# Ten value units as rounded halves and rests in place of four, and a new order of the last units

## The chip, the cores and the metric

The kernel runs on one core of a Trainium2 chip. The metric is device time in microseconds (us), here the median of several executions. The engines of the core each work through their own list of instructions and wait for one another by semaphores: TensorE (PE in the profile, its weight loads PEld), VectorE (DVE), ScalarE (ACT), GpSimd (POOL) and SyncE (SP), which here only issues DMAs.

## The reference

Self-attention over an image of 4 batches, 128 channels and 1024 positions, all in float32:

```
def _L0_conv_ref(x, gn_w, gn_b, qw, qb, kw, kb, vw, vb, pw, pb):
    h = _group_norm(x, gn_w, gn_b)                 # 8 groups
    q = jnp.einsum('oc,bcn->bon', qw, h) + qb[None, :, None]
    k = jnp.einsum('oc,bcn->bon', kw, h) + kb[None, :, None]
    v = jnp.einsum('oc,bcn->bon', vw, h) + vb[None, :, None]
    attn = jnp.einsum('bcn,bcm->bnm', q, k) / jnp.sqrt(jnp.asarray(C, x.dtype))
    attn = jax.nn.softmax(attn, axis=-1)
    out = jnp.einsum('bnm,bcm->bcn', attn, v)
    out = jnp.einsum('oc,bcn->bon', pw, out) + pb[None, :, None]
    return x + out.reshape(B, C, H, W)
```

## The kernel before, in words

The 4096 query positions are cut into 32 **chunks** of 128, eight to a batch. For chunk c, TensorE makes the scores against all 1024 keys of its batch (L329 to L333; both operands are split into a rounded half and a rest, hi and lo, so that one product takes three passes of the faster kind: hi by hi, hi by lo, lo by hi). VectorE copies them out of PSUM and finds the minimum of each row (L703, "drain"), ScalarE takes the exponential (L524), and the probabilities must then be transposed before they can be multiplied by v. For chunks 0, 1, 30 and 31 TensorE transposes them (L426). For the others VectorE transposes blocks of 32 by 32 (L712), and DMAs put the blocks in their places: a **set** of four chunks (`SETS`; sets 1 to 7) is moved by 16 DMAs of 128 KB from `blocks` to `pT` (L196), four for each of four groups a. The semaphore `moved[...][a]` counts the four of a group.

A moved set is multiplied by v in four **value units**. Units 0 and 1 make the first 256 columns (groups a = 0, 1), from key tiles 0 to 3 and 4 to 7; units 2 and 3 the other 256 (a = 2, 3). I write (n, u) for unit u of set n. A whole unit is four matmuls of 256 columns in float32 (L399), each of which the trace shows as two records. Sets 2, 4 and 6 cross from one batch to the next and are cut otherwise; their units are eight matmuls of 128 columns. In the main loop unit number m runs after the scores of chunk m + 8 (`LAG`). In this kernel (3, 2), (3, 3), (5, 2) and (5, 3) are **rounded units**: v and the probabilities are split into hi and lo, and twelve faster matmuls take the place of the four (L370 to L372). The halves come from ScalarE, which casts (`round_v` L533, `round_probs` L543), the rests from GpSimd, which subtracts (`split_v` L864, `split_probs` L872). `p_hi` and `p_lo` have room for two units.

After the loop, TensorE ends with units 23 to 25, the rden broadcast, (7, 0), (7, 1), then chunks 30 and 31 together in two direct units (L357), then (7, 2), (7, 3) (L473 to L480). VectorE multiplies each finished sum by the inverse denominators (`divide` L732, `finish_last_moved` L745 and L750, `add_residual` L738) and SP stores the rows. All of SP's transfers, the moves, the spreading of the inverse denominators and the stores, stand in one order (L225 to L237): for each set its move, its spread, and the store of the set two before.

## Time and profile before

| what | us |
|---|---|
| median of three runs | 140.52 (139.68 to 140.91) |
| the profiled execution | 139.28 |
| its span | 137.0 |
| TensorE busy | 128.5 (94%) |
| VectorE busy | 100.8 (74%) |
| ScalarE busy | 70.4 (51%) |
| GpSimd busy | 40.4 (29%) |

The span is what the trace covers; the profiled execution's own time is 2.28 us more. Busy time is an average over parts of the program with different limits. The chain of waits follows the end of the program back, from each piece of work to what released it.

### The profile page before, as it was taken

To read this page: it belongs to the slowest core of one execution; us is meant where nothing else is said; L and a number is where in the kernel's file an instruction comes from.
4 is the path that set the end of the run, shared out by engine and by line. 5 is a ranking of instruction groups with operands and counts; after the bars stand their busy time and mean duration, and the time that the engine had idled before them with its cause. 6 is when DMAs were issued, how large, how long until landed. Compare 5 with 4: busy or idle time off the path is not lost.

```text
span 137.0 us, 2258 instructions
## 1 busy us (share of the span) xinstructions
PE 128.5 (94%) x759; PEld 111.9 (82%) x759; DVE 100.8 (74%) x172; ACT 70.4 (51%) x118; POOL 40.4 (29%) x39
## 2 busy tenths in 40 slices
PE   5999999997877999999999999999999999999990
PEld 5897888884556888989898898899988999998870
DVE  0577789989999678979689989856987798240222
ACT  4053789655556574637357796475576335321000
POOL 5053050750202033303324696015039412003000
PEclk9999999999999999999999999999999999999999
DMA  4960000003998599869672898799835997999412
GB/s 139 288 263 0 0 5 0 10 31 67 202 212 195 136 208 208 181 150 208 136 188 105 195 212 196 221 206 208 198 105 120 199 209 219 237 206 199 153 38 77
DMA packets 9566, 21.00 MB, mean 153 GB/s; under 512 B 2362, under 2 KB 4052, under 8 KB 9556
## 3 DMA queue, kind: packets, MB, share of 16 engines
q1 hardware_dynamic: 8816, 20.59, 61.7%
q10 hardware_dynamic: 740, 0.28, 0.8%
q8 instruction: 6, 0.10, 0.3%
q14 instruction: 4, 0.03, 0.1%
HBM read 4.07 MB, written 2.11 MB: 45 GB/s over the span
## 4 chain that ended last, share of the span: by engine, by line
PE 84%; DVE 8%; issue 3%; DMA 2%; SPq 0%; DVEq 0%
PE ACC L399 31%; PE S L329 10%; PE S L330 9%; PE S L333 9%; PE A L309 5%; DVE s_sb L703 3%; PE S L357 3%; PE ACC L357 3%; DMA x_sb<-x 2%; PE S L273 2%; DVE blocks L712 2%; PE ACC L371 1%; DVE bn L628 1%; PE ACC L372 1%; PE ACC L370 1%
## 5 line engine op out<-in xcount | busy, mean ns | idle before, releaser
L703 DVE TENSOR_SCALAR_CACHE_REDUCE s_sb<-S,row_term 128x1024 f32<-128x1024 f32 x32 | 40.9, 1279 | 13.9 <-PE S L333 13.7
L399 PE MATMUL ACC<-pT,v 128*128 128x128 f32 (+1 forms) x288 | 45.8, 310 | 0.0
L524 ACT ACTIVATE s_sb<-s_sb,rowmin 128x1024 f32<-128x1024 f32 x32 | 36.9, 1152 | 15.6 <-DVE s_sb L703 14.1
L399 PEld LDWEIGHTS ACC<-pT,v 128*128 128x128 f32 x288 | 40.3, 191 | 3.2 <-issue 0.4
L712 DVE STREAM_TRANSPOSE blocks<-s_sb 128x1024 f32<-128x1024 f32 x28 | 34.7, 1239 | 0.0
L329 PE MATMUL S<-h_hi,g_hi 128*128 128x512 f32 x64 | 28.5, 446 | 0.3 <-issue 0.3
L330 PE MATMUL S<-h_lo,g_hi 128*128 128x512 f32 x64 | 25.1, 393 | 0.0
L333 PE MATMUL S<-h_hi,g_lo 128*128 128x512 f32 x64 | 19.9, 392 | 0.0
L857 POOL TENSOR_TENSOR xb<-rden_bc,xb 128x512 f32<-128x512 f32 (+1 forms) x7 | 8.4, 1200 | 26.5 <-DVE rden_bc L732 18.9
L333 PEld LDWEIGHTS S<-h_hi,g_lo 128*128 128x128 f32 x64 | 12.0, 188 | 2.8
L329 PEld LDWEIGHTS S<-h_hi,g_hi 128*128 128x128 f32 x64 | 12.1, 189 | 2.1 <-issue 0.4
L330 PEld LDWEIGHTS S<-h_lo,g_hi 128*128 128x128 f32 x64 | 12.1, 189 | 1.7
L872 POOL TENSOR_TENSOR p_lo<-pT,p_hi 128x1024 fp32r<-128x1024 f32 x4 | 9.6, 2403 | 10.2 <-ACT p_hi L543 10.2
L516 ACT COPY v<-A 128x384 f32<-128x384 f32 (+1 forms) x12 | 5.3, 443 | 14.2 <-PE A L309 14.2
L309 PEld LDWEIGHTS A<-wpv,h 128*128 128x128 f32 x64 | 8.4, 190 | 3.7 <-issue 2.6
L309 PE MATMUL A<-wpv,h 128*128 128x129 f32 x64 | 9.5, 281 | 1.3 <-DVE g_lo L677 1.2
L844 POOL TENSOR_TENSOR h_lo<-h,h_hi 128x1024 fp32r<-128x1024 f32 x3 | 7.2, 2402 | 11.7 <-ACT h L494 11.7
L504 ACT ACTIVATE g_hi<-A,wpv 128x512 fp32r<-128x512 f32 x7 | 4.8, 689 | 9.2 <-PE A L291 9.2
L273 PE MATMUL S<-ident 128*128 128x128 f32 x38 | 7.3, 343 | 1.6 <-POOL ident L877 1.6
L864 POOL TENSOR_TENSOR v_lo<-v,v_hi 128x1024 fp32r<-128x1024 f32 x2 | 4.7, 2368 | 12.8 <-ACT v_hi L533 12.8
L835 POOL TENSOR_TENSOR rstd<-gvar,minus_half 128x1 f32<-128x1 f32 x4 | 2.2, 554 | 20.2 <-DVE gvar L650 20.2
L628 DVE BATCH_NORM_STATS2 bn<-x_sb 128x6 f32<-128x512 f32 x8 | 5.3, 684 | 3.2 <-DMA x_sb<-x 3.2
(100 smaller groups left out, 144.7 us busy)
## 6 DMA issues: line engine op xcount, KB each, us to landing
pT<-blocks SPq DMA_DIRECT2D x112, 128.0 KB, 2.4
rden_bc<-row_store SPq DMA_DIRECT2D x6, 256.0 KB, 3.5
x_sb<-x SPq DMA_DIRECT2D x1, 1024.0 KB, 6.4
out<-xb SPq DMA_DIRECT2D x8, 128.0 KB, 2.8
out<-xb SPq DMA_DIRECT2D x4, 256.0 KB, 3.1
x_sb<-x SPq DMA_DIRECT2D x2, 256.0 KB, 3.0
x_sb<-x SPq DMA_DIRECT2D x1, 512.0 KB, 3.8
w_in<-weights ACTq DMA_DIRECT2D x2, 128.0 KB, 3.5
```

What stands on the lines that cost most here:

```text
L273: pe.matmul(S[:, 0, BANK:BANK + P], ident[:, :], ident[:, :], start=True, stop=True)
L309: last = pe.matmul(A1[:, PW1 * u:PW1 * (u + 1)], h[:, P * t:P * (t + 1)], wpv[:, 0:PW1], start=True, stop=True)
L329: pe.matmul(S[:, c % 2, ks], g_hi[:, qs], h_hi[:, b % 2, ks], start=True, stop=False)
L330: pe.matmul(S[:, c % 2, ks], g_hi[:, qs], h_lo[:, b % 2, ks], start=False, stop=False)
L333: last = pe.matmul(S[:, c % 2, ks], g_lo[:, qs], h_hi[:, b % 2, ks], start=False, stop=True)
L357: last = pe.matmul(sums[n], v[:, FIRST[n] // CH % 3, t, :], pair_T[:, t].rearrange("p d q -> p (d q)"), start=(t == 0), stop=(t == KT - 1))
L399: last = pe.matmul(to, v[:, b % 3, t, :], probs[:, :, t, :], start=(t == 0), stop=(t == KT - 1))
L524: act.activation(s_sb[:, c % 3, :], s_sb[:, c % 3, :], ACT.Exp, bias=rowmin[:, c % CH:c % CH + 1], scale=-1.0, accum_out=den[:, n % 2, k:k ...
L703: dve.tensor_scalar(s_sb[:, c % 3, :], S[:, c % 2, :], row_term[:, b % 2, i:i + 1], None, ALU.add, ALU.min, accum_out=rowmin[:, i:i + 1]). ...
L712: dve.transpose(blocks_view(n)[:, :, :, k, :].rearrange("p j t q -> p t j q"), s_sb[:, c % 3, :].rearrange("p (t j q) -> p t j q", t=KT, j ...
L857: pool.tensor_tensor(xs, rden_bc[:, n % 2, 0:P * SETS[n]], xs, ALU.add).then_inc(out_ready, 1)
L872: pool.tensor_tensor(lo, moved_view(n)[:, 2:4, PT * half:PT * (half + 1), :].rearrange("p a t n -> p t a n"), hi.bitcast(F32), ALU.subtrac ...
```

## The change

- The units that are rounded are now listed one by one (`SPLIT_UNITS`): (1, 2), (1, 3), (3, 0) and (5, 0) are new in the loop, (7, 2) and (7, 3) at the end; (3, 2), (3, 3), (5, 2), (5, 3) stay. v is split four times in place of two, by ScalarE after the exponentials of chunks 7, 15, 23 and 30 and by GpSimd a chunk later.
- ScalarE casts for (1, 2) and (1, 3) after the exponential of chunk 10, for (3, 0) and (5, 0) in chunks 17 and 25 ahead of the rounding of g, for (7, 2) and (7, 3) after all its other work. The rests for the last two are made by VectorE, not GpSimd.
- Chunks 30 and 31 get a unit each, of eight matmuls of 128 columns. The end is (7, 0), (7, 1), chunk 30, (7, 2), (7, 3), chunk 31. Each of the two chunks has its own two VectorE operations and its own store.

```diff
 FIRST_UNIT_STEPS = (4, 5)
 LAG = 8
 
-SPLIT_SETS = (3, 5)
+SPLIT_UNITS = ((1, 2), (1, 3), (3, 0), (3, 2), (3, 3), (5, 0), (5, 2), (5, 3), (7, 2), (7, 3))
+
+SPLIT_SETS = (1, 3, 5, 7)
+ROUND_V_STEPS = (7, 15, 23, 30)
+
+BY_DVE = 8
...
+
+    FIRST_QUARTERS = {FIRST[n] + 7: SPLIT_UNITS.index((n, 0)) for n in (3, 5)}
+    SECOND_QUARTERS = {FIRST[n] + 6 + u: SPLIT_UNITS.index((n, u)) for n in (3, 5) for u in (2, 3)}
...
-        sums = [ACC[:, n % 2, 0:P * SETS[n]] for n in range(LS)] + [S[:, 1, 0:PN]]
+        sums = [ACC[:, n % 2, 0:P * SETS[n]] for n in range(LS)]
+
+        chunk_sums = [S[:, 1, BANK * d:BANK * d + P] for d in range(2)]
...
+
+        def split_views(r):
+
+            n, u = SPLIT_UNITS[r]
+            part, half = u // 2, u % 2
+            probs = moved_view(n)[:, 2 * part:2 * (part + 1), PT * half:PT * (half + 1), :].rearrange("p a t n -> p t a n")
+            return (probs, *(p[:, r % 2].rearrange("p t (a n) -> p t a n", a=2) for p in (p_hi, p_lo)))
+
+        def unit_end(r):
+
+            n, u = SPLIT_UNITS[r]
+            return FIRST[n] + u + 1
...
-                    sp.wait_ge(tail_out_ready, 2 if n == LS else 3)
+                    sp.wait_ge(tail_out_ready, 3)
...
+            def store_chunk(d):
+                sp.wait_ge(tail_out_ready, (2, 4)[d])
+                cs = slice(P * (CH - 2 + d), P * (CH - 1 + d))
+                sp.dma_start(out[L, :, cs], xb[:, L, cs]).then_inc(stored, 16)
...
             store_set(LS - 2)
-            store_set(LS)
+            store_chunk(0)
             store_set(LS - 1)
-            sp.wait_ge(stored, 16 * (NS + sum(crosses(n) for n in range(NS))))
+            store_chunk(1)
+            sp.wait_ge(stored, 16 * (NS + 1 + sum(crosses(n) for n in range(NS))))
...
+            def last_chunk_unit(d):
+                for f in range(HALVES):
+                    pe.wait_ge(pair_ready[f], SETS[0] + SETS[LS])
+                pe.wait_ge(v_ready, VP * B)
+                pe.wait_ge(rowmin_ready, STEPS)
+                for t in range(KT):
+                    last = pe.matmul(chunk_sums[d], v[:, L % 3, t, :], pair_T[:, t, d, :], start=(t == 0), stop=(t == KT - 1))
+                last.then_inc(part_done, 1)
+
+            def split_unit(n, u):
+                r, k = SPLIT_UNITS.index((n, u)), SPLIT_SETS.index(n)
+                part, half = u // 2, u % 2
+                if u == 0:
+                    pe.wait_ge(normed_ready, n - 1)
+                if u == 2 and n == LS - 1:
+                    pe.wait_ge(normed_ready, n)
+                pe.wait_ge(v_hi_ready, k + 1)
+                pe.wait_ge(v_lo_ready, k + 1)
+                pe.wait_ge(p_hi_ready, r + 1)
+                if r < BY_DVE:
+                    pe.wait_ge(p_lo_ready, r + 1)
+                else:
+                    pe.wait_ge(last_lo_ready, r - BY_DVE + 1)
+                to = last_sums[part] if n == LS - 1 else sums[n][:, UW * part:UW * (part + 1)]
                 for w in range(PT):
                     t = PT * half + w
-                    pe.matmul(to, v_hi[:, t, :], p_hi[:, half, w, :], start=(t == 0), stop=False)
-                    pe.matmul(to, v_hi[:, t, :], p_lo[:, half, w, :], start=False, stop=False)
-                    last = pe.matmul(to, v_lo[:, t, :], p_hi[:, half, w, :], start=False, stop=(t == KT - 1))
+                    pe.matmul(to, v_hi[:, t, :], p_hi[:, r % 2, w, :], start=(t == 0), stop=False)
+                    pe.matmul(to, v_hi[:, t, :], p_lo[:, r % 2, w, :], start=False, stop=False)
+                    last = pe.matmul(to, v_lo[:, t, :], p_hi[:, r % 2, w, :], start=False, stop=(t == KT - 1))
                 last.then_inc(part_done, 1)
...
             def moved_unit(n, u):
-                if n in SPLIT_SETS and u > 1:
-                    split_unit(n, u - 2)
+                if (n, u) in SPLIT_UNITS:
+                    split_unit(n, u)
                     return
...
-                if n in (0, LS):
-                    direct_unit(n, u)
+                if n == 0:
+                    first_pair_unit(u)
+                elif n == LS:
+                    last_chunk_unit(u)
                 else:
                     moved_unit(n, u)
...
             value_unit(FIRST[LS - 1])
             value_unit(FIRST[LS - 1] + 1)
             value_unit(DIRECT)
-            value_unit(DIRECT + 1)
             value_unit(FIRST[LS - 1] + 2)
             value_unit(FIRST[LS - 1] + 3)
+            value_unit(DIRECT + 1)
...
+            def round_probs(r):
+                n, u = SPLIT_UNITS[r]
+                for a in (2 * (u // 2), 2 * (u // 2) + 1):
+                    act.wait_ge(moved[n % 2][a], MOVED * ((n + 1) // 2))
+                if r > 1:
+                    act.wait_ge(part_done, unit_end(r - 2))
+                    act.wait_ge(p_lo_ready, r - 1)
+                probs, hi, lo = split_views(r)
+                act.copy(hi, probs).then_inc(p_hi_ready, 1)
...
                 if i == 0:
                     copy_v(b, 1)
+                if c in FIRST_QUARTERS:
+                    round_probs(FIRST_QUARTERS[c])
                 if i == 1:
                     round_g(b, 1)
...
-                for k, n in enumerate(SPLIT_SETS):
-                    if c - FIRST[n] in (8, 9):
-                        round_probs(n, c - FIRST[n] - 8)
+                if c in SECOND_QUARTERS:
+                    round_probs(SECOND_QUARTERS[c])
                 exponentials(c)
-                for k, n in enumerate(SPLIT_SETS):
-                    if c == FIRST[n] + 5:
-                        round_v(k)
+                if c in ROUND_V_STEPS:
+                    round_v(ROUND_V_STEPS.index(c))
+                if c == FIRST[1] + LAG:
+                    round_probs(0)
+                    round_probs(1)
             copy_pair(STEPS - 1)
             copy_rden(LS - 1)
             copy_rden(LS)
+            round_probs(BY_DVE)
+            round_probs(BY_DVE + 1)
...
-                dve.wait_ge(part_done, FIRST[n] + SETS[n] if n < LS else STEPS - 2)
+                dve.wait_ge(part_done, FIRST[n] + SETS[n])
...
+            def finish_last_chunk(d):
+                dve.wait_ge(part_done, (STEPS - 3, STEPS)[d])
+                dve.wait_ge(bc_ready, 2)
+                by_rden = rden_bc[:, LS % 2, P * d:P * (d + 1)]
+                dve.tensor_tensor(by_rden, chunk_sums[d], by_rden, ALU.mult).then_inc(chunk_normed, 1)
+                dve.wait_ge(chunk_normed, d + 1)
+                dve.wait_ge(xb_ready, B)
+                xs = xb_flat[:, P * (DIRECT + d):P * (DIRECT + d + 1)]
+                dve.tensor_tensor(xs, by_rden, xs, ALU.add).then_inc(tail_out_ready, 1)
+
+            def split_last_probs(half):
+                r = BY_DVE + half
+                dve.wait_ge(p_hi_ready, r + 1)
+                dve.wait_ge(part_done, unit_end(r - 2))
+                probs, hi, lo = split_views(r)
+                dve.tensor_tensor(lo, probs, hi.bitcast(F32), ALU.subtract).then_inc(last_lo_ready, 1)
...
-                dve.wait_ge(part_done, FIRST[n] + 2 if part == 0 else STEPS)
+                dve.wait_ge(part_done, FIRST[n] + 2 if part == 0 else STEPS - 1)
...
             divide(LS - 2)
+            split_last_probs(0)
             finish_last_moved(0)
-            divide(LS)
-            add_residual(LS)
+            split_last_probs(1)
+            finish_last_chunk(0)
             finish_last_moved(1)
+            finish_last_chunk(1)
...
+            def split_probs(r):
+                pool.wait_ge(p_hi_ready, r + 1)
+                if r > 1:
+                    pool.wait_ge(part_done, unit_end(r - 2))
+                probs, hi, lo = split_views(r)
+                pool.tensor_tensor(lo, probs, hi.bitcast(F32), ALU.subtract).then_inc(p_lo_ready, 1)
...
-                for k, n in enumerate(SPLIT_SETS):
-                    if c == FIRST[n] + 6:
-                        split_v(k)
-                    if c - FIRST[n] in (8, 9):
-                        split_probs(n, c - FIRST[n] - 8)
+                if c - 1 in ROUND_V_STEPS:
+                    split_v(ROUND_V_STEPS.index(c - 1))
+                if c in FIRST_QUARTERS:
+                    split_probs(FIRST_QUARTERS[c])
+                if c in SECOND_QUARTERS:
+                    split_probs(SECOND_QUARTERS[c])
+                if c == FIRST[1] + LAG:
+                    split_probs(0)
+                    split_probs(1)
```

TensorE's rows from the broadcast of the inverse denominators (rden) to its last instruction, before: L399 are whole units of set 7, L357 chunks 30 and 31.

```order
L426 MATMUL A<-ident,s_sb 128x128 x8
L399 MATMUL ACC<-pT,v 128x2x64 x8
L347 MATMUL S<-ident,rden 128x128 x6
L399 MATMUL ACC<-pT,v 128x256 x8
L357 MATMUL S<-pair_T,v 128x256 x8
L399 MATMUL ACC<-pT,v 128x256 x8
```

The same place with the change (L444 are whole units, L395 a chunk, L415 to L417 rounded units).

```order
L473 MATMUL A<-ident,s_sb 128x128 x8
L444 MATMUL ACC<-pT,v 128x2x64 x8
L375 MATMUL S<-ident,rden 128x128 x6
L444 MATMUL ACC<-pT,v 128x256 x8
L395 MATMUL S<-pair_T,v 128x128 x8
L415 MATMUL ACC<-p_hi,v_hi 128x256
L416 MATMUL ACC<-p_lo,v_hi 128x256
L417 MATMUL ACC<-p_hi,v_lo 128x256
...
L395 MATMUL S<-pair_T,v 128x128 x8
```

Chunk 31 has moved behind the two last units of set 7, and these are rounded: the three rows L415 to L417 come eight times.

VectorE's last rows, from the division of set 6's sums, before (L745 and L750 finish a half of set 7, L729 and L738 the two chunks).

```order
L732 TENSOR_TENSOR rden_bc<-ACC,rden_bc 128x4x4x32
L745 TENSOR_TENSOR rden_bc<-ACC,rden_bc 128x2x4x32
L750 TENSOR_TENSOR xb<-rden_bc,xb 128x2x4x32
L729 TENSOR_TENSOR rden_bc<-S,rden_bc 128x256
L738 TENSOR_TENSOR xb<-rden_bc,xb 128x256
L745 TENSOR_TENSOR rden_bc<-ACC,rden_bc 128x2x4x32
L750 TENSOR_TENSOR xb<-rden_bc,xb 128x2x4x32
```

The same with the change (L801 makes a rest, L808 and L813 finish a half of set 7, L790 and L794 a chunk).

```order
L783 TENSOR_TENSOR rden_bc<-ACC,rden_bc 128x4x4x32
L801 TENSOR_TENSOR p_lo<-pT,p_hi 128x1024
L808 TENSOR_TENSOR rden_bc<-ACC,rden_bc 128x2x4x32
L813 TENSOR_TENSOR xb<-rden_bc,xb 128x2x4x32
L801 TENSOR_TENSOR p_lo<-pT,p_hi 128x1024
L790 TENSOR_TENSOR rden_bc<-S,rden_bc 128x128
L794 TENSOR_TENSOR xb<-rden_bc,xb 128x128
L808 TENSOR_TENSOR rden_bc<-ACC,rden_bc 128x2x4x32
L813 TENSOR_TENSOR xb<-rden_bc,xb 128x2x4x32
L790 TENSOR_TENSOR rden_bc<-S,rden_bc 128x128
L794 TENSOR_TENSOR xb<-rden_bc,xb 128x128
```

The first rest stands ahead of the finish of set 7's first half, the second behind it.

ScalarE's rows of chunks 10 to 12 with the change; before, the row of the two casts (L590) is not there.

```order
L571 ACTIVATE s_sb,den<-s_sb,rowmin 128x1024
L590 CAST p_hi<-pT 128x1024 x2
L536 ACTIVATE h_hi<-x_sb,gshift,gscale 128x1024
L571 ACTIVATE s_sb,den<-s_sb,rowmin 128x1024
L541 ACTIVATE h<-x_sb,gshift,gscale 128x1024
```

Both casts stand between the exponential of chunk 10 (L571) and the normalizing for the next batch (L536), which the exponential of chunk 11 follows.

## Rows read from the trace of the kernel before

**Rows 1.** The page, TensorE's busy tenths in 40 equal slices of the span.

```profile
PE   5999999997877999999999999999999999999990
```

**Rows 2.** Chain of waits, 111 to 137 us: start, us, engine and line, records.

```profile
112.17 1.78 PE ACC L399 x16
...
123.09 3.68 PE ACC L399 x16
126.77 3.45 PE S L357 x16
130.22 3.47 PE ACC L399 x16
133.71 0.44 DVE rden_bc L745
...
134.17 0.42 DVE xb L750
```

**Rows 3.** Timeline of SP's queue, 100 to 137 us: start, us, line, operation.

```profile
102.29 10.98 SPq L196 DMA_DIRECT2D pT<-blocks  x16
...
114.96 10.50 SPq L196 DMA_DIRECT2D pT<-blocks  x16
```

**Rows 4.** Timeline of VectorE, 100 to 118 us: transposes of chunks 25 and 29.

```profile
101.02 1.24 DVE L712 STREAM_TRANSPOSE blocks<-s_sb 128x1024 f32<-128x1024 f32 x1
...
113.55 1.24 DVE L712 STREAM_TRANSPOSE blocks<-s_sb 128x1024 f32<-128x1024 f32 x1
```

**Rows 5.** Set 7's moves: seventh and eighth, then fifteenth and sixteenth, with landings.

```profile
L196 SPq DMA_DIRECT2D pT<-blocks x2: 590/596/602, 118.8 to 119.5; - x2
DMA to landing us min/median/max: 2.9/3.2/3.5
...
L196 SPq DMA_DIRECT2D pT<-blocks x1: 592/592/592, 124.9 to 124.9; - x1
DMA to landing us min/median/max: 2.6/2.6/2.6
```

**Rows 6.** Timeline of TensorE, 100 to 118 us: starts of units (5,1), (5,2), (5,3).

```profile
103.28 1.89 PE L399 MATMUL ACC<-pT,v 128*128 128x256 f32 x8
...
106.40 0.28 PE L370 MATMUL ACC<-p_hi,v_hi 128*128 128x256 f32 x1
...
109.20 0.28 PE L370 MATMUL ACC<-p_hi,v_hi 128*128 128x256 f32 x1
```

**Rows 7.** Groups by line and shape: busy us and mean ns, idle before.

```profile
L543 ACT CAST p_hi<-pT 128x1024 fp32r<-128x1024 f32 x4 | 4.2, 1044 | 0.0
L668 DVE TENSOR_TENSOR h_lo<-h,h_hi 128x512 fp32r<-128x512 f32 x2 | 1.4, 709 | 0.4 <-ACT h_hi L489 0.4
```

**Rows 8.** Timeline of all engines, 73.5 to 82 us: start, us, engine, operation.

```profile
73.73 2.39 POOL L872 TENSOR_TENSOR p_lo<-pT,p_hi 128x1024 fp32r<-128x1024 f32 x1 [1.90 <-ACT p_hi L543]
...
74.42 1.72 DVE L661 SCALAR_TENSOR_TENSOR gshift<-neg_mean,gscale,cols 128x1 f32<-128x1 f32 x1
...
78.48 2.42 POOL L872 TENSOR_TENSOR p_lo<-pT,p_hi 128x1024 fp32r<-128x1024 f32 x1 [1.13 <-ACT p_hi L543]
...
81.28 0.28 PE L370 MATMUL ACC<-p_hi,v_hi 128*128 128x256 f32 x1
```

**Rows 9.** Timeline of ScalarE, 43 to 69 us; in brackets the idle time before.

```profile
45.27 1.24 ACT L489 ACTIVATE h_hi<-x_sb,gshift,gscale 128x1024 fp32r<-128x1024 f32 x1 [0.26 <-issue]
47.80 1.15 ACT L524 ACTIVATE s_sb<-s_sb,rowmin 128x1024 f32<-128x1024 f32 x1 [1.28 <-DVE s_sb L703]
...
68.48 0.69 ACT L504 ACTIVATE g_hi<-A,wpv 128x512 fp32r<-128x512 f32 x1 [2.19 <-PE A L291]
```

**Rows 10.** Timeline of SP's queue, 30 to 100 us: the moves of sets 1 and 3.

```profile
31.97 10.12 SPq L196 DMA_DIRECT2D pT<-blocks  x16
...
58.38 11.24 SPq L196 DMA_DIRECT2D pT<-blocks  x16
```

**Rows 11.** Busy time per engine, 34 to 42 us; granted clock, DMA share and GB/s last.

```profile
34.00:42.00 8.00, 6.39 (x30) 4.41 (x28) 7.97 (x16) 4.96 (x10) 0.74 (x1) 1.00 0.95 208
```

More of the change, by code:

```diff
@@ L349, in broadcast_rden, with first_pair_unit @@
                 last.then_inc(bc_psum, 1)
-            def direct_unit(n, half):
+            def first_pair_unit(half):
                 if half == 0:
                     for f in range(HALVES):
-                        pe.wait_ge(pair_ready[f], 2 if n == 0 else 4)
-                    pe.wait_ge(v_ready, VP if n == 0 else VP * B)
+                        pe.wait_ge(pair_ready[f], SETS[0])
+                    pe.wait_ge(v_ready, VP)
                 for t in range(PT * half, PT * (half + 1)):
-                    last = pe.matmul(sums[n], v[:, FIRST[n] // CH % 3, t, :], pair_T[:, t].rearrange("p d q -> p (d q)"),
+                    last = pe.matmul(sums[0], v[:, 0, t, :], pair_T[:, t].rearrange("p d q -> p (d q)"),
@@ L358, in direct_unit @@
                                      start=(t == 0), stop=(t == KT - 1))
                 last.then_inc(part_done, 1)
-            def split_unit(n, half):
-                k = 2 * SPLIT_SETS.index(n) + half
-                pe.wait_ge(v_hi_ready, k // 2 + 1)
-                pe.wait_ge(v_lo_ready, k // 2 + 1)
-                pe.wait_ge(p_hi_ready, k + 1)
-                pe.wait_ge(p_lo_ready, k + 1)
-                to = sums[n][:, UW:2 * UW]
+            def last_chunk_unit(d):
[6 more added lines that the diff above has]
+                last.then_inc(part_done, 1)
@@ L533, in round_v @@
                 act.copy(v_hi[:, :, :], v[:, b % 3]).then_inc(v_hi_ready, 1)
-            def round_probs(n, half):
-                k = 2 * SPLIT_SETS.index(n) + half
-                if half == 0:
-                    for a in (2, 3):
-                        act.wait_ge(moved[n % 2][a], MOVED * ((n + 1) // 2))
-                if k > 1:
-                    act.wait_ge(part_done, FIRST[SPLIT_SETS[k // 2 - 1]] + 2 + half + 1)
-                    act.wait_ge(p_lo_ready, k - 1)
-                act.copy(p_hi[:, half].rearrange("p t (a n) -> p t a n", a=2),
-                         moved_view(n)[:, 2:4, PT * half:PT * (half + 1), :].rearrange("p a t n -> p t a n")).then_inc(p_hi_ready, 1)
+            def round_probs(r):
[7 more added lines that the diff above has]
+                act.copy(hi, probs).then_inc(p_hi_ready, 1)
             def copy_rows(n):
```

18 lines of the change are left out of this document (3 added, 15 removed).

## The prediction, made before the changed kernel ran

> **What bounds the kernel now.** I read the page's busy slices of TensorE first: nine tenths or more in every slice of 3.4 us from 44.5 us to the end of its work, seven or eight in the four before that [rows 1]. The chain of waits over the last 25 us says where this decides: after the scores of chunk 31 it is TensorE alone, value unit after value unit, and then two VectorE operations and a store [rows 2]. So a microsecond taken from TensorE is a microsecond gained wherever TensorE is what everybody waits for, and nothing where it waits itself. The profiled execution took 139.28 us, 2.28 more than its span of 137.0; the median of the three runs is 140.52, 1.24 above it. I make the sum in the trace's own time and add 3.5 at the end.
>
> Two other views matter. The SP queue shows that the moves of set 7 are issued from 114.96 on, directly behind those of set 6 and its other transfers: 102.29 to 114.96, or 12.67 us, of which the moves alone take 10.98; the last blocks of set 7 are ready at 113.55 + 1.24 = 114.79 [rows 3, 4]. SP and VectorE are level there. And the moves' landings: the eighth DMA of set 7 (issued 119.46) lands after 3.5 us, at 122.96; unit 26, which needs the first eight, has its first matmul on the chain at 123.09 [rows 2, 5]. So the moves are already level with TensorE. The sixteenth (issued 124.87) lands after 2.6, at 127.47 [rows 5]; TensorE reaches unit 28, which needs it, only at 130.22. These 2.75 us of slack are what the change spends.
>
> **A rounded unit against a whole one.** Unit and next scores of a whole quarter take 106.40 - 103.28 = 3.12 us; with a rounded one 109.20 - 106.40 = 2.80 [rows 6]. So **0.32 us per unit** on TensorE. Six more are rounded: (1,2), (1,3), (3,0), (5,0) in the loop, (7,2), (7,3) at the end. Each costs ScalarE a cast of 1.04 and a subtraction on GpSimd of 2.4 (at the end: on VectorE) [rows 7, 8]. The two more roundings of v cost the same two instructions, behind the exponentials of chunks 7 and 30. There ScalarE's next work, a copy for TensorE or VectorE, comes up to 1 us later; both have work of their own until then, VectorE at chunk 7 and TensorE at chunk 30, so I count 0, and 1.04 once if that cover fails.
>
> **Loop, early.** (1,2) and (1,3) run after the scores of chunks 12 and 13, in full slices [rows 1]. Their casts stand behind the exponential of chunk 10 and ahead of the h_hi that ScalarE starts at 45.27 [rows 9]; set 1's moves have then landed (issued from 31.97 over 10.12 [rows 10], the last at 41.5, landing by 44.1). The casts put h_hi and the exponential of chunk 11 back: 45.0 + 2 x 1.04 + 1.24 = 48.3, against a start of that exponential at 47.80 [rows 9], so 0.5, of which VectorE, which transposes chunk 11 only after draining chunk 12, sees nothing. I count this at 0 and the saving at 0.64; without the cover it would be the 0.5.
>
> **Loop, sets 3 and 5.** Each first quarter's cast stands before the rounding of g, where ScalarE sits idle 2.19 us before set 3's at 68.48 [rows 9] (set 5 repeats it, two such places in all); 1.04 fits, if the first eight moves have landed, which by start + 8.0 (as in set 7: 114.96 to 122.96) is 66.4 for set 3, against 68.48 - 1.04 = 67.4. The covered cost is 0; without that cover, chunk 17's exponential would be late by up to 1 us. One place is tight. The subtraction for (3,2) already blocks VectorE: the one-column gshift takes 1.72 us beside GpSimd's 2.39, and both end near 76.1 [rows 8]. Behind it stand the cast and subtraction for (3,3), ready at 78.48 + 2.42 = 80.90; TensorE wants it at 81.28 [rows 8]. The first of these subtractions can move up by 0.64 only (chunk 17's gain), TensorE by 0.96: 80.26 against 80.32. That costs 0 to 0.1.
>
> The Trainium skill, "SBUF — State Buffer", section "Who interferes with whom", says that a VectorE instruction with two SBUF inputs waits for a GpSimd one that reads SBUF, and one with a single SBUF input, outside the two-port modes, doesn't. The gshift row agrees with the first half; no row shows g_lo (one input in PSUM) beside a subtraction. By the page the new subtraction at chunk 17 costs g_lo nothing; if it were wrong, g_lo would wait the 0.4 by which the two overlap in my schedule.
>
> So by chunk 26 VectorE is ahead by 3 x 0.32 = **0.96**, by chunk 30 by 1.28.
>
> **Set 7's moves.** Its blocks are ready at 114.79 - 1.28 = 113.51. SP began set 6's moves when chunk 25 was transposed (101.02 + 1.24 = 102.26 [rows 4]), now at 101.33, and needs its 12.67: 114.00. So the moves gain 0.96, TensorE 1.28. Unit 26 waits for the eighth until 122.96 - 0.96 = 122.0. Units 26 and 27 as before, 3.68 [rows 2], to 125.8. Chunk 30 as eight 128-column matmuls: as the eight (16 passes) of 1.78 [rows 2], to 127.6. The two chunks take 3.57 where the pair took 3.45: 0.12 more.
>
> **The end.** Unit (7,2) could start at 127.6. Its cast needs all 16 moves: **L = 127.47 - 0.96 = 126.5** (ScalarE has by then only its two rden copies to make, for which TensorE's part ended at 123.1 - 1.28). From L on the work is serial:
> - cast, 1.04 [rows 7];
> - subtraction on VectorE. No row has it at 1024 columns. Bounds: 1.24, the transpose of 1024 [rows 4], and 2 x 0.709 = 1.42, the 512-column one with both inputs in SBUF doubled [rows 7]. I take 1.25, since the fixed part of an instruction isn't doubled;
> - (7,2) can start: L + 2.4 = 128.9, a **TensorE stall of 1.3**. It ends 1.42 later, at 130.3;
> - but VectorE must first finish the first half of set 7, queued behind the first subtraction: 0.44 + 0.42 [rows 2], then the second subtraction, 1.25: L + 4.55 = 131.0, a second stall of 0.7;
> - unit (7,3) 1.42 (half of the last pair's 3.47 [rows 2] less 0.32), chunk 31 1.79: 134.3;
> - two VectorE operations of 128 columns. The 256-column ones take 0.44 and 0.42; 512 takes 0.709, so 128 columns fewer are 0.14 less: 0.60 with the handoff. VectorE ends at 134.9, where it ended at 134.59;
> - the last store: 137.0 - 134.59 = 2.41, taken unchanged, since nothing shows a 64 KB one. It could be a few tenths less.
>
> In all: handoffs 0.15, L + 1.04 + 1.25 + 0.88 + 1.25 + 1.42 + 1.79 + 0.60 + 2.41 = L + 10.79 = **137.3**, against 137.0: +0.3. What was gained by chunk 26 (0.96), with the two rounded units and the shorter finish, is spent by the wait on the cast and two subtractions. In run time 139.28 + 0.3 = 139.6, at the median **140.8**.
>
> The store of set 7 is issued at about 133.4 and lands before the last. SP's new store of chunk 30 stands before it and waits for VectorE at 131.6, so holds up nothing.
>
> The bounds of L: issue of 16 moves from 10.12 to 11.24 in other sets against 10.50 [rows 3, 10], start between 113.5 (bound by the blocks) and 114.0: L from 125.6 to 127.3. With 0 to 0.3 from the two subtractions that is 136.4 to 138.4, in runs **139.9 to 141.9**: the forecast's own range.
>
> **Rivals.**
> - *The end does not wait.* Were moves, cast and subtraction early enough, TensorE would run through: 122.0 + 3.68 + 1.79 + 2 x 1.42 + 1.79 = 132.1, + 3.01 = 135.1, so -1.9: **138.6**. For it: the end is otherwise pure TensorE, ScalarE and VectorE are idle there, and the landing times are the least sure of my numbers. Against: L must be at most 125.2 for no first stall and 124.5 for no second, 2 us earlier than the trace has it. A half of the way would do for -0.9. 0.18.
> - *Slower: the loop gives nothing by chunk 29.* The new casts sit ahead of exponentials, and subtractions beside gshift. If the casts of chunks 10, 17 and 25 put back VectorE's transposes by 0.32 each, the 0.96 is gone, VectorE and SP start set 7's moves at 114.96, and with 11.24 of issue L = 114.96 + 10.65 + 2.6 = 128.2, the end at 139.0: +2.0, **142.5**. It decides from L = 127.6 on (that is +1.4). For: the 0.1 of room at (3,3), and the 0.5 at chunk 11. Against: ScalarE has 2 us idle at the other two places. 0.13.
> - *The clock falls at the stall.* Then (7,3) and chunk 31 go at 1.2 GHz, +3.2: **144.0**. Against: from 34 to 42 us TensorE was busy only 6.39 of 8 us, and the granted clock stayed at 1.00 (2.4 GHz) [rows 11]. The Trainium skill, "TensorE: Matmul & The Clock Gate", section "HAM oscillation — how this bites in real kernels", says that waits between bursts bring the clock down; this stretch does not show it. 0.04.
> - That the change doesn't do what it says can be left out: the rounded unit exists already and its price is measured.
>
> **Numbers.** Forecast 0.65, no-wait 0.18, slower loop 0.13, clock 0.04. One per cent, 1.4 us, is about what can be told from no change. Faster by more (under 139.1): most of the no-wait case, 0.16. Slower by more (over 141.9): the loop and the clock cases and a tail of the forecast, 0.16. Same: 0.68. The range reaches down to the no-wait case and up to the border of the slow one: 138.7 to 142.1.
>
> **What would show it.** Chunks with the new rounded units 2.80 apart; set 7's first move near 114.0; the sixteenth landing near 126.5; a VectorE wait on the cast; TensorE idle 1.3 and then 0.7 us before (7,2) and (7,3), released by VectorE; chunk 31's last operation near 134.9. I am wrong if TensorE has no gap there (then the time is near 138.6), or if set 7's moves begin at 114.9 (then near 141.9 or above).

## The result: 0.7% faster, where no change was forecast

| | us, median | ratio to before |
|---|---|---|
| before, 20 runs | 140.27 (139.18 to 140.91) | |
| changed, 20 runs | 139.25 (138.44 to 140.92) | 0.9931 [0.9909, 0.9953] |

Five of the changed kernel's twenty executions (140.55 to 140.92 us) count as slow and are left out of the ratio; in four of them the mean granted clock was 0.988, which some 3.3 us at 1.2 GHz would give, and as no trace of them was kept, it is open whether the clock fell at the stall.

The forecast was 140.8, which is 0.3 us or 0.2% above the 140.52 of the three runs that it started from. Measured is a gain of 1.0 us, by more than the measurement leaves open. The time lies in the range, and the forecast's mechanism, a wait at the end that spends what the loop gains, stands in the trace. What failed are two terms behind it: the last store, taken as 2.41 us and measured at 2.02, and the time outside the span, taken as 2.28 and measured at 1.73.

The two profiled executions can't be compared by their absolute times. VectorE's first drain, the end of the work on the weights, starts at 13.19 us before and at 14.31 in the changed kernel. The timelines of VectorE show it, before and changed (start, us, engine, line, operation):

```profile
13.19 1.28 DVE L703 TENSOR_SCALAR_CACHE_REDUCE s_sb<-S,row_term 128x1024 f32<-128x1024 f32 x1 [0.24 <-PE S L333]
```

```profile
14.31 1.28 DVE L754 TENSOR_SCALAR_CACHE_REDUCE s_sb<-S,row_term 128x1024 f32<-128x1024 f32 x1 [0.24 <-PE S L361]
```

The change touches nothing ahead of this point, and other kernels below have it anywhere from 13.45 to 14.25. So I take every time from the start of that drain (**at equal head**): a time t of before is t - 13.19, one of the changed kernel t - 14.31. Ends of spans are the traces' own to a hundredth, 137.04 and 137.99, which the profile rounds to 137.0 and 138.0.

### The end of the changed kernel

SP's queue in the changed kernel (start, us, line, operation), to be held against [rows 3]:

```profile
102.57 10.06 SPq L218 DMA_DIRECT2D pT<-blocks  x16
...
114.75 10.56 SPq L218 DMA_DIRECT2D pT<-blocks  x16
125.36 1.57 SPq L238 DMA_DIRECT2D out<-xb  x3
132.28 0.33 SPq L244 DMA_DIRECT2D out<-xb  x1
134.48 0.33 SPq L238 DMA_DIRECT2D out<-xb  x1
136.00 0.33 SPq L244 DMA_DIRECT2D out<-xb  x1
```

VectorE's transpose of chunk 29, which makes the last blocks of set 7, in its timeline [rows 4]:

```profile
113.48 1.24 DVE L763 STREAM_TRANSPOSE blocks<-s_sb 128x1024 f32<-128x1024 f32 x1
```

The chain of waits that ended last, in order of time (start, us, what):

```profile
124.72 2.71 DMA pT<-blocks
127.43 0.03 ACTq L588
127.45 0.04 issue
127.49 1.05 ACT p_hi L590
128.55 0.02 issue
128.57 0.04 DVE p_lo L801
...
129.71 0.43 DVE rden_bc L808
...
130.51 1.23 DVE p_lo L801
131.74 0.14 issue
131.87 0.36 PE ACC L415
```

Where [rows 2] had nothing but TensorE from unit 26 on, the chain now runs through the sixteenth move, ScalarE's cast, VectorE's rest of (7,2), the finish of set 7's first half, the rest of (7,3). TensorE's timeline shows what that does to it (L444 units 26 and 27, L395 a chunk, L415 the first matmul of a rounded unit; in brackets its idle time and what ended it):

```profile
122.87 3.62 PE L444 MATMUL ACC<-pT,v 128*128 128x256 f32 x16
126.32 1.95 PE L395 MATMUL S<-pair_T,v 128*128 128x128 f32 x16
129.94 0.36 PE L415 MATMUL ACC<-p_hi,v_hi 128*128 128x256 f32 x1 [1.67 <-DVE p_lo L801]
...
131.87 0.36 PE L415 MATMUL ACC<-p_hi,v_hi 128*128 128x256 f32 x1 [0.26 <-DVE p_lo L801]
...
133.37 1.95 PE L395 MATMUL S<-pair_T,v 128*128 128x128 f32 x16
```

And VectorE's:

```profile
128.57 1.23 DVE L801 TENSOR_TENSOR p_lo<-pT,p_hi 128x1024 fp32r<-128x1024 f32 x1 [5.46 <-ACT p_hi L590]
129.71 0.42 DVE L808 TENSOR_TENSOR rden_bc<-ACC,rden_bc 128x256 f32<-128x256 f32 x1
130.16 0.42 DVE L813 TENSOR_TENSOR xb<-rden_bc,xb 128x256 f32<-128x256 f32 x1
130.51 1.22 DVE L801 TENSOR_TENSOR p_lo<-pT,p_hi 128x1024 fp32r<-128x1024 f32 x1
...
135.68 0.29 DVE L794 TENSOR_TENSOR xb<-rden_bc,xb 128x128 f32<-128x128 f32 x1
```

VectorE had been idle for 5.46 us before the first of these: it had time, and nothing to subtract from.

### What was forecast and what the trace has, at equal head

| | forecast | changed | before |
|---|---|---|---|
| set 7's moves start | 100.81 | 100.44 | 101.77 |
| unit 26, first matmul | 108.81 | 108.56 | 109.90 |
| sixteenth move lands (L) | 113.31 | 113.12 | 114.28 |
| (7,2), first matmul | 115.71 | 115.63 | |
| (7,3), first matmul | 117.81 | 117.56 | |
| VectorE's last operation ends | 121.71 | 121.66 | 121.40 |
| span ends | 124.11 | 123.68 | 123.85 |
| the run's time outside the span | 2.28 | 1.73 | 2.24 |

The forecast's column is its own times less 13.19. At VectorE's last operation it is right within 0.05 us, in part by luck: the moves start 0.37 earlier than forecast and (7,3) 0.25 earlier, but from there to VectorE's end it takes 4.10 us and not 3.90. The last two rows are off by 0.43 and 0.55, in the same direction.

### The profile page after: what moved, and what is told of

Its sections match the earlier page's. It is cut to its first block, busy times and chain, and to the rows that moved or that the text cites. A ratio compares the mean times of both kernels' runs of the same rounds, so it can differ in the third digit from the quotient of the medians.

```text
span 138.0 us, 2392 instructions
## 1 busy us (share of the span) xinstructions
PE 128.4 (93%) x799; PEld 113.3 (82%) x799; DVE 103.2 (75%) x176; ACT 77.8 (56%) x126; POOL 54.6 (40%) x45
## 4 chain that ended last, share of the span: by engine, by line
PE 71%; DVE 11%; SPq 7%; issue 6%; DMA 2%; ACT 1%; POOL 0%; DVEq 0%; POOLq 0%; ACTq 0%
PE ACC L444 16%; PE S L357 9%; PE S L358 9%; PE S L361 9%; SPq L218 7%; PE S L301 5%; PE A L337 5%; DVE s_sb L754 4%; PE ACC L415 3%; PE ACC L417 3%; PE ACC L416 3%; DVE blocks L763 3%; PE ACC L385 3%; DMA pT<-blocks 2%; PE S L395 1%
## 5 line engine op out<-in xcount | busy, mean ns | idle before, releaser
L571 ACT ACTIVATE s_sb<-s_sb,rowmin 128x1024 f32<-128x1024 f32 x32 | 36.8, 1151 | 12.6 <-DVE s_sb L754 11.0
L444 PE MATMUL ACC<-pT,v 128*128 128x128 f32 (+1 forms) x240 | 34.6, 296 | 0.0
L444 PEld LDWEIGHTS ACC<-pT,v 128*128 128x128 f32 x240 | 31.3, 191 | 1.8
L357 PE MATMUL S<-h_hi,g_hi 128*128 128x512 f32 x64 | 27.7, 433 | 0.3 <-issue 0.3
L936 POOL TENSOR_TENSOR p_lo<-pT,p_hi 128x1024 fp32r<-128x1024 f32 x8 | 19.1, 2394 | 11.5 <-ACT p_hi L590 11.5
L929 POOL TENSOR_TENSOR v_lo<-v,v_hi 128x1024 fp32r<-128x1024 f32 x4 | 9.5, 2376 | 22.4 <-ACT v_hi L580 22.4
L357 PEld LDWEIGHTS S<-h_hi,g_hi 128*128 128x128 f32 x64 | 12.1, 189 | 2.0 <-issue 0.4
L415 PE MATMUL ACC<-p_hi,v_hi 128*128 128x256 f32 x40 | 11.6, 291 | 1.9 <-DVE p_lo L801 1.9
L590 ACT CAST p_hi<-pT 128x1024 fp32r<-128x1024 f32 x10 | 10.2, 1042 | 2.8 <-DMA pT<-blocks 2.6
L416 PE MATMUL ACC<-p_lo,v_hi 128*128 128x256 f32 x40 | 11.2, 281 | 0.0
L417 PE MATMUL ACC<-p_hi,v_lo 128*128 128x256 f32 x40 | 11.2, 281 | 0.0
L415 PEld LDWEIGHTS ACC<-p_hi,v_hi 128*128 128x128 f32 x40 | 7.5, 188 | 2.8 <-issue 2.6
```

Source lines behind the costliest of these rows:

```text
L357: pe.matmul(S[:, c % 2, ks], g_hi[:, qs], h_hi[:, b % 2, ks], start=True, stop=False)
L415: pe.matmul(to, v_hi[:, t, :], p_hi[:, r % 2, w, :], start=(t == 0), stop=False)
L416: pe.matmul(to, v_hi[:, t, :], p_lo[:, r % 2, w, :], start=False, stop=False)
L417: last = pe.matmul(to, v_lo[:, t, :], p_hi[:, r % 2, w, :], start=False, stop=(t == KT - 1))
L444: last = pe.matmul(to, v[:, b % 3, t, :], probs[:, :, t, :], start=(t == 0), stop=(t == KT - 1))
L571: act.activation(s_sb[:, c % 3, :], s_sb[:, c % 3, :], ACT.Exp, bias=rowmin[:, c % CH:c % CH + 1], scale=-1.0, accum_out=den[:, n % 2, k:k ...
```

## The experiments

Each was compared with the kernel before, run on the same chip. Unless said otherwise an edit is against the changed kernel.

### e1: the two roundings of set 7 left out

```diff
-SPLIT_UNITS = (..., (5, 2), (5, 3), (7, 2), (7, 3))
+SPLIT_UNITS = (..., (5, 2), (5, 3))
...
-            round_probs(BY_DVE)
-            round_probs(BY_DVE + 1)
...
-            split_last_probs(0)
...
-            split_last_probs(1)
```

The rounding of v for set 7 goes with them.

> The changed kernel without the rounding of (7,2) and (7,3): eight rounded units in the loop and the new order of the end stay. Theory A (the end of the changed kernel hangs on the landing of set 7's sixteenth move, then cast and two subtractions, and the rounding of these two units spends more than it saves): TensorE has no gap after unit 26, the trace ends about 1.2 us before the kernel before (135.8 against 137.0 at equal start) and about 1 us before the changed kernel; ratio to before 0.990 to 0.992. Theory B (the measured gain of 1.0 us comes from the end's rounding and order, not from the loop): the time lies at or above the changed kernel's, ratio 0.995 to 1.0.

Measured 137.55 us, ratio **0.9844 [0.9811, 0.9877]**, clear of the changed kernel's interval. The direction is the expected one, the size is not: 0.990 to 0.992 was expected, and the span is 1.77 us shorter than the changed kernel's at equal head where 1 was. TensorE runs through the end:

```profile
122.37 3.62 PE L444 MATMUL ACC<-pT,v 128*128 128x256 f32 x16
125.83 1.95 PE L395 MATMUL S<-pair_T,v 128*128 128x128 f32 x16
127.61 3.62 PE L444 MATMUL ACC<-pT,v 128*128 128x256 f32 x16
131.07 1.95 PE L395 MATMUL S<-pair_T,v 128*128 128x128 f32 x16
```

VectorE's last operation ends 1.76 us earlier than in the changed kernel at equal head. The two roundings take 0.64 us from TensorE's work and cost 1.76 at the end.

### e2 and e3: the loop alone, the order alone

e2 keeps only the four new rounded units of the loop, with before's end. e3 keeps only the new order with the chunks' own operations and stores.

```diff
 e3
-SPLIT_UNITS = ((1, 2), (1, 3), (3, 0), (3, 2), (3, 3), (5, 0), (5, 2), (5, 3), (7, 2), (7, 3))
+SPLIT_UNITS = ((3, 2), (3, 3), (5, 2), (5, 3))
...
-            round_probs(BY_DVE)
-            round_probs(BY_DVE + 1)
...
-            split_last_probs(0)
...
-            split_last_probs(1)
```

> Only the four new rounded units (1,2), (1,3), (3,0), (5,0) and the rounding of v for them; the end as before the change. Theory A: set 7's first move starts 1.0 to 1.3 us earlier and so does everything behind it, ratio 0.991 to 0.993. Theory B: TensorE's gain is lost at unit 26, which waits for the moves, ratio 0.998 to 1.0.

> Only the new order of the end with a unit and a store for each of chunks 30 and 31; rounded units as before the change. Theory A: 0.12 us more on TensorE, 0.26 less on VectorE at the end, so -0.15, ratio 0.998 to 1.0; if the last store of 64 KB is shorter, up to 0.3 more. Theory B: -0.5 or more, ratio 0.996 or less.

e2: 138.03 us, ratio **0.9878 [0.9845, 0.9911]**. e3: 139.6 us, ratio **0.9979 [0.9953, 1.0005]**. So the loop alone gives more than the whole change (the two intervals only just touch, and e2's span is 1.2 us the shorter at equal head), and more than the 0.991 to 0.993 expected; the order alone gives at most little. e3 also isolates the last store: VectorE ends 0.16 us later than before at equal head, and the span is 0.28 shorter. From VectorE's end to the span's end it is 2.45 us in before and 2.0 with a chunk's own store of 64 KB. The last stores by line, before (two of 256 KB) and then changed (one of 64 KB):

```profile
L216 SPq DMA_DIRECT2D out<-xb x2: 332/332/332, 131.2 to 134.6; - x2
DMA to landing us min/median/max: 1.9/1.9/2.0
```

```profile
L244 SPq DMA_DIRECT2D out<-xb x1: 332/332/332, 136.0 to 136.0; - x1
DMA to landing us min/median/max: 1.6/1.6/1.6
```

### e4: (7,3) rounded, (7,2) whole

```diff
-SPLIT_UNITS = (..., (7, 2), (7, 3))
+SPLIT_UNITS = (..., (7, 3))
...
-            round_probs(BY_DVE + 1)
...
+            finish_last_moved(0)
             split_last_probs(0)
-            finish_last_moved(0)
-            split_last_probs(1)
```

> The changed kernel with (7,2) left whole, (7,3) still rounded, its subtraction behind the finish of set 7's first half. Theory A: (7,2) needs only the landing, so TensorE has no first stall; cast and subtraction for (7,3) lie beside it, and the second stall is at most 0.2. The end is 1.3 to 1.5 us earlier than in the changed kernel's trace at equal start, ratio to before 0.988 to 0.990. Theory B: about as the changed kernel, 0.993.

Measured 137.35 us, ratio **0.9831 [0.9802, 0.986]**. That is more than the 0.988 to 0.990 expected. One rounding at this place costs next to nothing, since a whole (7,2) covers its cast and rest:

```profile
128.10 1.89 PE L444 MATMUL ACC<-pT,v 128*128 128x256 f32 x8
129.91 0.36 PE L415 MATMUL ACC<-p_hi,v_hi 128*128 128x256 f32 x1
```

No idle time stands before the second row, but only just: the rest ends at 129.77. VectorE ends 0.14 us earlier than in e1; 0.32 were to be had. The difference to e1 in the ratio is within both intervals.

### e5: both rests before the finish of the first half

```diff
             split_last_probs(0)
-            finish_last_moved(0)
             split_last_probs(1)
+            finish_last_moved(0)
```

> The changed kernel, with VectorE making both of its rests before it finishes the first half of set 7 (in the changed kernel the finish stands between them). Theory (the end is one serial line from the landing of set 7's sixteenth move: cast, rest, unit (7,2), rest, unit (7,3), chunk 31): the second stall (0.26 us) goes and (7,3) starts as soon as (7,2) is done; VectorE's last operation 0.3 to 0.5 us earlier than in the changed kernel at equal head, ratio to before 0.990 (0.988 to 0.993). The first stall of TensorE (1.67) stays. Rival (TensorE's end is bound by something else than the rests, such as the spacing of its own units): no change, 0.993. The reported time that stands outside the span stays near the changed kernel's 1.7 us.

Measured 138.61 us, ratio **0.9892 [0.9858, 0.9925]**; the interval overlaps the changed kernel's, so the time alone would not decide. TensorE's timeline does: the first stall is there (1.76), the second is gone, and VectorE ends 0.35 us earlier at equal head.

```profile
129.36 0.36 PE L415 MATMUL ACC<-p_hi,v_hi 128*128 128x256 f32 x1 [1.76 <-DVE p_lo L801]
...
130.86 0.28 PE L415 MATMUL ACC<-p_hi,v_hi 128*128 128x256 f32 x1
```

### e6 and e10: other work in the wait

e6 puts chunk 31 ahead of (7,2). e10 takes back the new order altogether (the pair together, one store), with all ten units rounded.

```diff
 e6
             value_unit(DIRECT)
+            value_unit(DIRECT + 1)
             value_unit(FIRST[LS - 1] + 2)
             value_unit(FIRST[LS - 1] + 3)
-            value_unit(DIRECT + 1)
...
```

VectorE's finishes and SP's stores follow in the same order.

> The changed kernel with chunk 31 ahead of (7,2) in place of at the very end: TensorE ends with chunk 30, chunk 31, (7,2), (7,3), and the last store is the 256 KB one of set 7. Both units stay rounded. Theory (chunk 31 put last left TensorE with nothing to do while cast and rest were made): chunk 31's 1.79 us fill the wait; in the changed kernel's times chunk 30 ends 128.1, chunk 31 129.9, (7,2) 130.0 to 131.5, (7,3) 131.8 to 133.2, VectorE's last operation 134.1 against 135.97; from there the larger store takes 2.4 in place of 2.0: span 1.5 shorter than the changed kernel's at equal head, ratio to before 0.983 (0.981 to 0.986). Rival (the wait follows the landing in any order, as the rounding is on the path whatever stands before it): 0.993, as the changed kernel. Rival (own store of chunk 31 at the end is what pays): slower than the changed kernel by 0.4 us, 0.996.

> All ten rounded units, with the old order of the end: (7,0), (7,1), the pair of chunks 30 and 31 together, then (7,2), (7,3) rounded, one store for the pair. Only the new order and the own stores of the chunks are taken back. Theory (a serial line from the landing of the sixteenth move): in the changed kernel's times the pair ends at 130.0, where the rest of (7,2) is ready at 129.9; (7,2) to 131.5, (7,3) to 133.3 at best, VectorE's last operation 134.1, a 256 KB store at the end: as with chunk 31 put ahead of (7,2), ratio to before 0.983 to 0.987. Rival (own stores and chunk 31 last are what gains in the changed kernel): 0.993 or above.

e6: 138.35 us, ratio **0.9871 [0.9831, 0.9911]**; a little less than expected, though its trace is as expected (span 1.45 us shorter than the changed kernel's at equal head, 1.5 expected). e10: 138.1 us, ratio **0.9858 [0.9827, 0.9889]**, as expected. In both the wait before (7,2) is gone; in e10 it is 0.24 before (7,3):

```profile
130.83 0.36 PE L410 MATMUL ACC<-p_hi,v_hi 128*128 128x256 f32 x1 [0.24 <-DVE p_lo L796]
```

So the new order, worth a little by itself (e3), costs time together with the new roundings: e10 differs from the changed kernel in nothing else, and their intervals don't meet. It moved the one piece of work that needs no move, chunk 31, out of the place where it would have covered the cast and the rest.

### e7 and e8: round the half that has landed

e7 rounds (7,0) and (7,1) in place of (7,2) and (7,3), with chunks 30 and 31 ahead of them. e8 rounds (7,3) too.

```diff
 e7
-SPLIT_UNITS = (..., (5, 3), (7, 2), (7, 3))
+SPLIT_UNITS = (..., (5, 3), (7, 0), (7, 1))
...
+            value_unit(DIRECT)
+            value_unit(DIRECT + 1)
             value_unit(FIRST[LS - 1])
             value_unit(FIRST[LS - 1] + 1)
-            value_unit(DIRECT)
             value_unit(FIRST[LS - 1] + 2)
             value_unit(FIRST[LS - 1] + 3)
-            value_unit(DIRECT + 1)
...
```

ScalarE makes the two casts ahead of its last rden copy, VectorE both rests ahead of all the finishes, and the stores follow the units.

> As many rounded units as in the changed kernel, but of set 7 the first half, (7,0) and (7,1), whose moves have landed early, in place of (7,2) and (7,3); VectorE makes their rests; TensorE ends with chunk 30, chunk 31, (7,0), (7,1) rounded, (7,2), (7,3) whole, and stores follow in that order. Theory: casts and rests of the landed half are made while chunks 30 and 31 are multiplied, so TensorE has no gap over 0.3 us after chunk 30's first matmul; in the changed kernel's times chunks 122.9 to 126.4, (7,0) and (7,1) to 129.3, (7,2) and (7,3) to 132.7, VectorE's last operation 133.6, span 136.05: 1.9 shorter at equal head, ratio to before 0.981 (0.978 to 0.984). Rival (casts and subtractions anywhere in the tail delay TensorE): a gap of 1 us or more before (7,0), ratio 0.988 to 0.993.

> As e7_landed_half, with (7,3) rounded as well: three rounded units of set 7. Theory: the sixteenth move lands at about 127.4 in the changed kernel's times, cast and rest of (7,3) are ready at about 130.0, and TensorE gets to (7,3) at 131.0, so this rounding is covered: VectorE's last operation at 133.3, span 0.3 shorter than e7's, 0.4 shorter than with (7,3) alone rounded (e4_only_73): ratio to before 0.979 (0.976 to 0.982), the fastest of all. Rival (VectorE, which now makes three rests and four finishes in a row, becomes what the end waits for): no better than e4_only_73, 0.983 or above, with TensorE waiting before (7,3).

e7: 137.45 us, ratio **0.9802 [0.9764, 0.984]**. e8: 136.93 us, ratio **0.9772 [0.9739, 0.9805]**, the lowest of all, though its interval overlaps e7's and just touches e4's. TensorE's timeline of e8 has no wait from unit 23 to the end; its last whole unit and the first matmul of (7,3):

```profile
128.55 1.89 PE L444 MATMUL ACC<-pT,v 128*128 128x256 f32 x8
130.09 0.47 PE L415 MATMUL ACC<-p_hi,v_hi 128*128 128x256 f32 x1
```

VectorE makes the first two rests while chunks 30 and 31 are multiplied, and the third ends at 129.75, ahead of need:

```profile
123.67 2.36 DVE L804 TENSOR_TENSOR p_lo<-pT,p_hi 128x1024 fp32r<-128x1024 f32 x2 [1.31 <-ACT p_hi L592]
...
128.53 1.22 DVE L804 TENSOR_TENSOR p_lo<-pT,p_hi 128x1024 fp32r<-128x1024 f32 x1 [1.44 <-ACT p_hi L592]
```

e8's span is 0.3 us shorter than e7's at equal head, as expected, but only 0.1 shorter than e4's, where 0.4 was expected. Two rounded units of set 7 cost 1.76 us at VectorE's end behind the sixteenth landing (changed against e1) and gain 0.35 behind the eighth (e7 against e1).

### e9: a control

The kernel before, written in the changed kernel's code with its tables and its end set back.

> Control: the kernel before, written in the changed kernel's code with its table set back (four rounded units, v split twice, chunks 30 and 31 as a pair, old order). Same instructions on every engine as before, other line numbers. Theory: ratio to before 1.000 (0.997 to 1.003), time outside the span 2.2 us as before; so the experiments' differences are of the parts and not of the rewriting. Rival (the time outside the span, 2.2 before and 1.7 to 1.9 in the kernels with ten or fewer loop roundings, belongs to how the code is written): 1.7 to 1.9 here too, ratio 0.997.

Measured 140.58 us, ratio **1.0015 [0.9983, 1.0048]**, and 2.2 us outside the span: the rewriting changes nothing. Its trace shows something that the profiled execution of before did not. TensorE waits for set 7's moves at unit 26:

```profile
124.29 3.69 PE L439 MATMUL ACC<-pT,v 128*128 128x256 f32 x16 [0.62 <-DMA pT<-blocks]
```

### All of them side by side

| kernel | first drain | set 6's moves take | set 7's moves start | VectorE ends | span | outside the span | ratio |
|---|---|---|---|---|---|---|---|
| before | 13.19 | 10.98 | 101.77 | 121.40 | 123.85 | 2.22 | |
| e9 | 13.79 | 11.31 | 102.08 | 122.02 | 124.46 | 2.22 | 1.0015 |
| e3 order | 13.47 | 10.81 | 101.66 | 121.56 | 123.57 | 2.20 | 0.9979 |
| changed | 14.31 | 10.06 | 100.44 | 121.66 | 123.68 | 1.74 | 0.9931 |
| e5 | 13.57 | 10.05 | 100.52 | 121.31 | 123.32 | 1.72 | 0.9892 |
| e2 loop | 13.45 | 10.04 | 100.46 | 120.01 | 122.46 | 1.95 | 0.9878 |
| e6 | 13.62 | 10.05 | 100.45 | 119.80 | 122.23 | 1.71 | 0.9871 |
| e10 | 13.49 | 10.05 | 100.49 | 119.93 | 122.37 | 1.71 | 0.9858 |
| e1 | 13.77 | 10.36 | 100.49 | 119.90 | 121.91 | 1.92 | 0.9844 |
| e4 | 14.25 | 10.04 | 100.50 | 119.76 | 121.77 | 1.96 | 0.9831 |
| e7 | 13.80 | 10.03 | 100.47 | 119.55 | 121.98 | 1.76 | 0.9802 |
| e8 | 13.55 | 10.03 | 100.46 | 119.24 | 121.67 | 1.74 | 0.9772 |

The second column is in the trace's time, the third is a length, the fourth to sixth are at equal head, the seventh is the median over the runs of (time less span). Wherever the loop has its four new rounded units, set 7's moves start within 100.44 to 100.52, and without them at 101.66 or later. That is the loop's gain, 1.2 us against e3, 1.3 against before and 1.6 against e9; what the kernels differ in besides is the end and the time outside the span.

## Why the prediction was wrong, step by step

- **The rounded unit, the casts, the loop.** Right. The cast of a new first quarter fits in ScalarE's idle time, the new casts at chunk 10 delay no drain, and the tight place at (3,3) costs about the 0.1 that was allowed: GpSimd's rest ends at 78.96 + 2.41 = 81.37, the first matmul comes right behind it at 81.52, and VectorE's drains, 0.96 ahead at chunk 21, are 0.84 ahead at chunk 26 and 1.18 at chunk 30 (0.96 and 1.28 were forecast). gshift still takes 1.71 us beside GpSimd. The subtraction for (3,0) ends at 67.81 + 2.38 = 70.19, and g_lo starts at 70.66: they never overlapped, so my doubt about g_lo was not put to the test.
- **"So the moves gain 0.96".** Undersized: they start 1.33 us earlier at equal head. I had VectorE 1.28 ahead but SP bound by set 6's moves, 10.98 us long. They took 10.06. In the view of set 6's sixteen issues, before, e3, e9 and then changed (ns, minimum, median and maximum):

```profile
L196 SPq DMA_DIRECT2D pT<-blocks x16: 513/592/1543, 102.3 to 112.7; - x16
DMA to landing us min/median/max: 2.4/2.4/3.5
```

```profile
L218 SPq DMA_DIRECT2D pT<-blocks x16: 513/592/1369, 102.6 to 112.8; - x16
```

```profile
L218 SPq DMA_DIRECT2D pT<-blocks x16: 513/591/1872, 102.9 to 113.6; - x16
```

```profile
L218 SPq DMA_DIRECT2D pT<-blocks x16: 512/592/607, 102.6 to 112.0; - x16
DMA to landing us min/median/max: 2.3/2.4/2.5
```

  The typical issue takes 0.59 us; before has one of 1.54, with a landing of 3.5, and the changed kernel has none there. This is no delay of one execution: all three kernels without the loop's new roundings have a long issue in set 6 (1.54, 1.37, 1.87), and of the nine with them eight have none over 0.61 and e1 has one of 0.91. So the long issue went with the change, and I had carried it over. Why it goes no run shows. In the changed kernel the moves start when the blocks are ready (113.48 + 1.24 = 114.72, first issue 114.75), which is 1.19 earlier than before; the other 0.14 is SP's. Set 7's own moves then take 10.56 in place of 10.50 and the last landing 2.71 in place of 2.6, so L gained 1.16 of the 1.33.
- **The serial end.** Right, and it is what the experiments confirm. I gave "L + 2.4" to (7,2); measured 129.94 - 127.43 = 2.51. "L + 4.55" to (7,3); measured 4.44. The stalls were forecast at 1.3 and 0.7. TensorE's records have it idle for 1.67 and 0.26; from start to start, as the forecast counts (a chunk 1.79, a rounded unit 1.50 as in e5), the waits are 1.83 and 0.43, since TensorE came to the first 0.6 us earlier than I thought. The VectorE rest at 1.25 was 1.23. e1, e5, e6 and e10 each take away one part of the chain (the roundings, the finish between the rests, the order); in the trace e5, e6 and e10 give back what was expected of that part, e1 1.77 us where 1 was expected.
- **"The last store: 2.41, taken unchanged ... It could be a few tenths less."** This failed by 0.4 us: 2.02 with the 64 KB store (135.97 to 137.99), against 2.45 before. e3 shows it alone. I named the possibility and left it out of the sum and out of the forecast's own bounds.
- **"I make the sum in the trace's own time and add 3.5 at the end."** This failed by another 0.5. Of the 3.5, 2.28 is the time outside the span, and that does not stay the same when the kernel changes: 2.2 in before, e3 and e9 (four rounded units), 1.92 to 1.96 in e1, e2 and e4 (eight, eight and nine), 1.71 to 1.76 in the rest (ten or eleven). It goes down as units are rounded. e9 excludes that the way the code is written does it. Why the roundings do it stays open; no view of the trace covers it.

- **The base.** The median of before over three runs was 140.52; over twenty it is 140.27. Of the 1.55 us between the forecast's 140.8 and the measured 139.25, 0.25 is this and not the change.

Together: +0.26 at VectorE's end, -0.43 for the store, -0.51 outside the span, -0.68 in all, where I had +0.3. Measured -0.97 (-1.28 to -0.66). The rest, 0.3, stays open. For it speaks that TensorE reaches unit 26's first matmul 0.81 us after the rden broadcast starts in before, 0.96 in e3 and 1.44 in e9, against 0.66 in the changed kernel: without the loop's gain it waits there for set 7's moves, and in before's profiled execution less than in the two others. Against it speaks that the same sum, for each kernel its profiled time less its first drain, held against before's, is off by as much in both directions elsewhere (us):

| | e1 | e2 | e3 | e4 | e5 | e6 | e7 | e8 | e9 | e10 |
|---|---|---|---|---|---|---|---|---|---|---|
| sum | -2.2 | -1.8 | -0.3 | -2.4 | -1.0 | -2.1 | -2.3 | -2.7 | +0.6 | -2.0 |
| measured | -2.2 | -1.7 | -0.3 | -2.4 | -1.5 | -1.8 | -2.8 | -3.2 | +0.2 | -2.0 |

A sum from one execution of each kernel is good to about 0.5 us here, and the 0.3 lies within that.

The rivals. *The end does not wait*: false for this kernel, true for e1, where the span is 1.94 us shorter than before at equal head: the price I gave the case, 1.9, was about right. *The loop gives nothing*: false, set 7's moves start 1.33 earlier. *The clock falls at the stall*: false in the profiled execution. The windows view of the changed kernel over the stretch with both stalls (columns: window, its us, busy us of PE, PEld, DVE, ACT, POOL, granted clock, DMA share, GB/s):

```profile
126.00:134.00 8.00, 6.07 (x49) 5.68 (x48) 4.04 (x7) 1.99 (x2) 0.00 (x0) 1.00 0.30 90
```

TensorE was busy 6.07 of 8 us, against 6.39 in [rows 11], and the granted clock is 1.00 (2.4 GHz); from the second matmul on, those behind the stalls take 0.28 as elsewhere. The section of the Trainium skill quoted in the forecast ("TensorE: Matmul & The Clock Gate", "HAM oscillation — how this bites in real kernels") has longer waits between the bursts of its example than the 1.67 us here, so this trace neither bears it out nor speaks against it.

## What to carry to other kernels

Making an engine's operation cheaper by preparing its operands elsewhere adds that preparation behind the operand's arrival: where the operand is the last thing to arrive, price cast plus subtraction plus handoffs against the slack, and spend the saving on operands that have already landed, with work that needs none of them placed in between. Every term of a sum needs its own row, the constant ones too: a last store of another size (0.4 us) and the time outside the span (0.5) together come to nearly the whole 1.0 us measured here. When cutting a change into its parts, look for the pair of parts that hurt each other; here both the roundings of set 7 with the old order (e10) and the new order without them (e1) beat the two together.
